# Moving two filler matmuls to another place within a step of the first attention's loop

## The chip, the cores and the metric

The kernel is written for one Trainium2 chip and runs on one of its cores. The metric is the device time of one execution in microseconds (us), and the figure for a kernel is the median of several executions. A profile is one further execution, recorded by the hardware profiler. The five engines named in it are TensorE (PE for its matmuls, PEld for its weight loads), VectorE (DVE), ScalarE (ACT), GpSimd (POOL) and SyncE (SP), which only issues transfers here. TensorE runs at one of two clock levels, 1.2 or 2.4 GHz. The profile gives the level that was granted as a share of the full one (1.00 or 0.50, or a mean of the two over a stretch).

## The reference

The reference is a decoder of two layers on 8 sequences of 128 tokens with 128 features. Each layer is a self-attention, a cross-attention to a context of 120 tokens, and a mixture of experts, each followed by a residual sum and a layer norm. The change is in the very first of these six parts, a differential attention with 16 heads of 8 features. Cut to what matters:

```
qkv = einsum('bnc,dc->bnd', x, W_qkv) split into q1, q2, k1, k2 (rotary) and v
attn1 = einsum('bhid,bhjd->bhij', q1, k1) * scale          # 8 sequences, 16 heads, 128 x 128
attn2 = einsum('bhid,bhjd->bhij', q2, k2) * scale
probs = softmax(attn1) - lam * softmax(attn2)
out   = einsum('bhij,bhjd->bhid', probs, v)                # then W_proj, residual, layer norm
```

## The kernel before

Nothing is scheduled by a planner. Each engine has its own program, written out by hand, and the engines meet at counting semaphores: an instruction adds to one when it ends, and another engine's program waits until the count is reached. What stands behind a wait on an engine's queue stands still with it.

The first attention works in 16 steps ("head numbers" n, 0 to 15). A step is a group of 16 score blocks of 128 x 128: four heads by four sequences, the four heads in the four 32-row quarters of TensorE. The names and lines that matter on TensorE's queue, in the order of one round n of the loop in `heads` (the function is printed below):

- `scores_t(n)` (lines 646 and 649): the transposed scores of step n, 16 matmuls of keys by queries (32 rows each) and 16 that add the row maxima. It waits until two score banks are free again (for the second, until DVE has taken the first half of the maxima of step n+2), and until ACT has copied the maxima of step n into `mT` (semaphore `mc`).
- `head_token(n-2)` (line 685): four 128 x 128 transposes of the finished outputs of step n-2 into the bank `BANK_M`.
- `head_values(n-1, 0)`: in the kernel before, first two fillers (line 607, in `keep_busy`), then the first eight matmuls of probabilities by values (line 673) into the bank `BANK_V`.
- `scores(n+2)` (line 633): the scores of step n+2 in the other orientation, 16 matmuls of 32 rows, from which DVE takes the row maxima.
- `head_maxima(n+1)` (line 660): one 128 x 128 transpose of the maxima of step n+1 into `BANK_M`.
- `head_values(n-1, 1)` (line 673): the second eight value matmuls.

A filler is a matmul of a 128 x 128 matrix of ones with 512 columns of ones (bf16). Its result is overwritten and used by nobody. In this loop only the first attention (`A`) has them; the second one (`D`), which runs through the same function later, adds masks with 128-row matmuls of 512 columns (line 622) instead.

The other engines in a round: DVE takes the row maxima in two halves (line 1318), cuts off their high bits (line 1326) and, in `finish_a` (lines 1342 to 1350), divides the outputs that `head_token` brought, which counts up `div`. POOL computes the low bits (line 506) and copies the values of a step (line 501). ACT runs, in this order, the two halves of the exponentials of step n, the copy of the maxima of step n+1 (into `mT`, counting up `mc`), and the copy of the outputs of step n-1 out of `BANK_V` (`outT`, counting up `ot`); all of ACT's work carries line 1072. SP loads queries and keys of later steps, eight steps ahead.

The last rounds differ: from n = 14 there are no `scores` left, from n = 15 no `head_maxima`, and the two rounds n = 16 and 17 only finish the outputs. Behind the loop `finish` issues five fillers of its own and goes on to the projection.

Of the kernel before, what the change touches and what calls it, by code (L numbers as in the profile page):

```python
# [48 lines left out]
BANK_V, BANK_M = 6, 7  # L49
# [80 lines left out]
def decoder_kernel(nc, d, out):  # L130
    with ExitStack() as ctx:
# [105 lines left out]
        def bank(n, k=1):  # L237
            return ps[:, n, :] if k == 1 else ps[:, n:n + k, :].rearrange("p a b -> p (a b)")
# [73 lines left out]
        A, D = Heads("a", 0), Heads("d", NH // RING)  # L312
# [288 lines left out]
        def _(pe):  # L601
            mm = nc.tensor.matmul

            def keep_busy(count, at):

                for _ in range(count):
                    mm(bank(at), onesb[:], fill, start=True, stop=True)  # L607
# [17 lines left out]
            def scores(a, n, causal):  # L625

                q, k = queries_of[n % RING], keys_of[n % RING]
                banks = head_banks(a, "s", n, causal, causS)
                for b in range(4):
                    cols = slice(b * P, (b + 1) * P)  # L630
                    for j in range(4):
                        rows = slice(QUAD * j, QUAD * j + QUAD)
                        last = mm(banks[j][:, cols], q[rows, cols], k[rows, cols], start=not causal, stop=not causal or b == 3)  # L633
                        if b == 3 and j % 2 == 1:
                            last.then_inc(a.s, 1)

            def scores_t(a, n, causal):

                q, k = queries_of[n % RING], keys_of[n % RING]
                banks = head_banks(a, "t", n, causal, causT)  # L640
                pe.wait_ge(a.mc, n + 1)
                for b in range(4):
                    cols = slice(b * P, (b + 1) * P)
                    for j in range(4):
                        rows = slice(QUAD * j, QUAD * j + QUAD)
                        mm(banks[j][:, cols], k[rows, cols], q[rows, cols], start=not causal, stop=False)  # L646
                    for j in range(4):
                        rows = slice(QUAD * j, QUAD * j + QUAD)
                        last = mm(banks[j][:, cols], pick[rows, b, :], mT[rows, n % 2, :], start=False, stop=not causal or b == 3)  # L649
                        if b == 3 and j % 2 == 1:  # L650
                            last.then_inc(a.st, 1)

            def head_maxima(a, n):

                pe.wait_ge(a.msplit, n + 1)
                if n >= 1:
                    pe.wait_ge(a.mc, n)
                if n >= 3:
                    pe.wait_ge(a.div, n - 2)
                nc.tensor.transpose(maxima_bank, mparts[:, n % 2].rearrange("p a b -> p (a b)"), ident).then_inc(a.mt, 1)  # L660

            def head_values(a, n, part):

                if part == 0:
                    pe.wait_ge(a.vs, n + 1)
                    if n >= 1:
                        pe.wait_ge(a.ot, n)
                    if a is A:
                        keep_busy(2, BANK_V)
                pe.wait_ge(a.exp, 2 * n + part + 1)  # L670
                for t in range(8 * part, 8 * part + 8):
                    j, k = divmod(t, 4)
                    last = mm(bank(BANK_V)[32 * k:32 * k + 32, j * P:(j + 1) * P], vs[:, n % 2, t, :], probs[:, n % 2, t, :],  # L673
                              start=True, stop=True)
                if part == 1:
                    last.then_inc(a.pv, 1)

            def head_token(a, n, count):

                pe.wait_ge(a.ot, n + 1)  # L680
                pe.wait_ge(a.mc, min(n + 3, count))
                if n >= 1:
                    pe.wait_ge(a.div, n)
                for k in range(4):
                    last = nc.tensor.transpose(bank(BANK_M)[:, k * P:(k + 1) * P], outT[:, k * P:(k + 1) * P], ident)  # L685
                last.then_inc(a.to, 1)

            def heads(a, count, causal):

                def loaded(n):  # L690
                    pe.wait_ge(a.stack[n % RING], (a.turns + n // RING + 1) * 16 * LOADS)

                for n in range(2):
                    loaded(n)
                    scores(a, n, causal)
                head_maxima(a, 0)
                for n in range(count + 2):
                    if n < count:
                        scores_t(a, n, causal)
                    if n >= 2:  # L700
                        head_token(a, n - 2, count)
                    if 0 <= n - 1 < count:
                        head_values(a, n - 1, 0)
                    if n + 2 < count:
                        loaded(n + 2)
                        scores(a, n + 2, causal)
                    if n + 1 < count:
                        head_maxima(a, n + 1)
                    if 0 <= n - 1 < count:
                        head_values(a, n - 1, 1)  # L710

            def finish(a, chunks, w):

                keep_busy(5, BANK_T)
                pe.wait_ge(a.norm, PAIRS)
                per = 4 // chunks
                banks = (BANK_S, BANK_S + 1, BANK_T, BANK_T + 1)
                for g in range(B // per):
                    for k in range(per):
                        for c in range(chunks):  # L720
                            o = bank(banks[g])[:, (k * chunks + c) * P:(k * chunks + c + 1) * P]
                            last = nc.tensor.transpose(o, oall[:, g * per + k, c * P:(c + 1) * P], ident)
                    last.then_inc(a.post, 1)
                for half in range(2):
                    pe.wait_ge(a.postc, (half + 1) * B // per // 2)
                    for k in range(4):
                        b = 4 * half + k
                        for c in range(chunks):
                            last = mm(bank(BANK_O + half)[:, k * P:(k + 1) * P], oT[:, b, c, :],
                                      w[:, c, :] if chunks == 2 else w[:],  # L730
                                      start=c == 0, stop=c == chunks - 1)
                    last.then_inc(a.y, 1)
# [44 lines left out]
            pe.wait_ge(fixed, 6)  # L777
            pe.wait_ge(tables, 5)
            heads(A, NH, causal=False)
            finish(A, 2, wproj0)  # L780
            keep_busy(10, BANK_T)
# [104 lines left out]
            pe.wait_ge(D.vall, 2)  # L886
            pe.wait_ge(D.full, 2)
            heads(D, PAIRS, causal=True)
            finish(D, 1, woD)

# [836 lines left out]
```

## Time and profile before

| | |
|---|---|
| three runs | 556.35, 557.04 and 563.35 us; median 557.04 us |
| profiled execution | 562.62 us, its span 560.8 us |
| mean granted clock over the span | 0.919 |
| busy share of the span | PE 87%, PEld 62%, DVE 50%, ACT 39%, POOL 18% |
| chain that ended last | PE 71%, DVE 18%, ACT 4%, DMA 2%, issue 2%, POOL 1% |

The profiled execution lies 5.58 us above the median, so a sum made in its own trace is made against 562.62 us. The chain that ended last is followed back from the last instruction: at each step to what released it, or to the instruction before it on the same engine. "Issue" is time in which an engine waited for nothing that the profile shows. The granted clock is read beside the busy share: TensorE can be busy all the time and yet work at half its speed.

### The profile page before, as it was taken

To read this page: it belongs to the slowest core of one execution; us is meant where nothing else is said; L and a number is where in the kernel's file an instruction comes from. 1 tells how busy PE (TensorE), PEld (TensorE's weight loads), DVE (VectorE), ACT (ScalarE), POOL (GpSimd) and SP (SyncE) were. 2 spreads that over 40 slices of the span, in tenths; PEclk is the share of its full clock that TensorE was granted. 3 is DMA by queue.
4 is the path that set the end of the run, shared out by engine and by line. 5 is a ranking of instruction groups with operands and counts; after the bars stand their busy time and mean duration, and the time that the engine had idled before them with its cause. 6 is when DMAs were issued, how large, how long until landed. Compare 5 with 4: busy or idle time off the path is not lost.

```text
span 560.8 us, 11515 instructions
## 1 busy us (share of the span) xinstructions
PE 487.8 (87%) x4512; PEld 347.0 (62%) x4512; DVE 283.2 (50%) x662; ACT 221.0 (39%) x359; POOL 101.5 (18%) x143
## 2 busy tenths in 40 slices
PE   8669988887689986789985899999998999999994
PEld 3456666664538953345563677777787667777774
DVE  2954566616764253334435966666614343333336
ACT  1324566641313300125432566666650643333330
POOL 2820112443100031000005222222221000000001
PEclk9865899998869998569997999999999999999998
DMA  7786430040400005700010000001000011111110
GB/s 202 254 289 212 137 107 2 3 152 0 151 0 1 1 1 213 255 6 3 2 40 12 12 13 13 13 21 28 2 1 1 20 28 39 38 38 38 38 28 37
DMA packets 23897, 34.36 MB, mean 61 GB/s; under 512 B 6400, under 2 KB 14544, under 8 KB 23600
## 3 DMA queue, kind: packets, MB, share of 16 engines
q1 hardware_dynamic: 23856, 33.77, 18.7%
q8 instruction: 31, 0.51, 0.4%
q14 instruction: 10, 0.08, 0.1%
HBM read 26.95 MB, written 6.82 MB: 60 GB/s over the span
## 4 chain that ended last, share of the span: by engine, by line
PE 71%; DVE 18%; ACT 4%; DMA 2%; issue 2%; POOL 1%; SPq 0%; POOLq 0%; DVEq 0%; ACTq 0%
PE ps L1024 10%; PE ps L1007 10%; PE ps L923 5%; DVE negm L1318 5%; PE ps L622 4%; PE ps L633 3%; PE ps L673 3%; PE ps L646 3%; PE ps L896 3%; PE ps L685 3%; PE ps L995 3%; PE ps L649 2%; PE ps L904 2%; PE ps L607 2%; PE ps L912 2%
## 5 line engine op out<-in xcount | busy, mean ns | idle before, releaser
L1318 DVE TENSOR_REDUCE negm<-ps 128x8 f32<-128x1024 f32 x48 | 56.5, 1219 | 55.1 <-PE ps L633 55.1
L1650 DVE SCALAR_TENSOR_TENSOR racc<-ps,sm,racc 128x128 f32<-128x128 f32 x128 | 35.9, 344 | 63.2 <-PE ps L1024 63.1
L1072 ACT ACTIVATE arena<-ps,w1a 128x512 f32<-128x512 f32 x64 | 43.4, 687 | 59.0 <-PE ps L1007 57.8
L1072 ACT ACTIVATE probs<-ps 128x1024 f32<-128x1024 f32 (+2 forms) x52 | 48.9, 989 | 39.7 <-PE ps L649 39.3
L1024 PEld LDWEIGHTS ps<-w1a,arena 128*128 128x128 f32 x512 | 59.4, 192 | 7.2 <-issue 6.2
L1024 PE MATMUL ps<-w1a,arena 128*128 128x128 f32 x512 | 59.8, 275 | 0.8 <-DVE racc L1641 0.8
L1007 PE MATMUL ps<-xT,w1a 128*128 128x512 f32 x128 | 58.0, 594 | 1.4 <-ACT xT L1072 1.4
L1072 ACT ACTIVATE arena<-ps 128x512 f32<-128x512 f32 (+4 forms) x62 | 35.1, 574 | 43.1 <-PE ps L831 15.8
L586 POOL TENSOR_TENSOR probs<-probs,rzE 128x480 f32<-128x480 f32 x32 | 30.6, 987 | 76.0 <-DVE rzE L1588 76.0
L545 POOL TENSOR_SCALAR rstd<-mv 128x4 f32<-128x4 f32 x12 | 2.7, 227 | 223.1 <-DVE mv L1379 223.1
L607 PE MATMUL ps<-onesb 128*128 128x512 bf16 x134 | 38.5, 424 | 3.0 <-DVE sm L1510 2.1
L1007 PEld LDWEIGHTS ps<-xT,w1a 128*128 128x128 f32 x128 | 23.0, 190 | 24.4 <-issue 22.2
L923 PEld LDWEIGHTS ps<-arena 128*128 128x128 f32 x256 | 30.4, 192 | 7.8 <-ACT arena L1072 4.2
L923 PE MATMUL ps<-arena 128*128 128x120 f32 x256 | 33.2, 278 | 1.6 <-ACT arena L1072 0.8
L673 PE MATMUL ps<-probs,vs 128*32 128x128 f32 x768 | 32.7, 296 | 0.0
L1575 DVE TENSOR_REDUCE negm<-ps 128x4 f32<-128x480 f32 x32 | 20.9, 654 | 20.8 <-PE ps L923 20.7
L506 POOL TENSOR_TENSOR mparts<-negm,mparts 128x64 f32<-128x64 f32 x24 | 7.7, 320 | 125.9 <-DVE mparts L1326 125.9
L649 PE MATMUL ps<-mT,pick 32*128 32x128 f32 x384 | 27.7, 306 | 0.0
L673 PEld LDWEIGHTS ps<-probs,vs 128*32 128x32 f32 x768 | 19.6, 115 | 12.1 <-issue 8.0
L1072 ACT ACTIVATE mT<-ps 128x128 fp32r<-128x128 f32 x24 | 6.7, 278 | 50.1 <-PE ps L660 50.1
L1072 ACT ACTIVATE probs<-probs 128x480 f32<-128x480 f32 x34 | 19.7, 600 | 13.1 <-DVE probs L1577 7.9
L1072 ACT ACTIVATE xT<-ps 128x512 f32<-128x512 f32 x10 | 6.0, 597 | 47.5 <-PE ps L738 47.4
(191 smaller groups left out, 836.3 us busy)
## 6 DMA issues: line engine op xcount, KB each, us to landing
stacks<-arena SPq DMA_DIRECT2D x12, 512.0 KB, 3.7
near<-stacks SPq DMA_DIRECT2D x12, 256.0 KB, 3.5
near<-stacks SPq DMA_DIRECT2D x24, 128.0 KB, 3.4
late<-stacks SPq DMA_DIRECT2D x12, 256.0 KB, 3.6
late<-stacks SPq DMA_DIRECT2D x24, 128.0 KB, 3.5
w1a<-in_w1a SPq DMA_DIRECT2D x1, 2048.0 KB, 7.5
w2a<-in_w2a SPq DMA_DIRECT2D x1, 2048.0 KB, 7.6
w1a<-in_w1b SPq DMA_DIRECT2D x16, 128.0 KB, 2.0
```

The lines of the kernel that those rows point to most:

```text
L586: nc.gpsimd.tensor_tensor(weights, weights, along(rzE[:, slot, 4 * g:4 * g + 4], L), ALU.mult).then_inc(e_norm, 1)
L607: mm(bank(at), onesb[:], fill, start=True, stop=True)
L622: mm(tiles(o, 4, P), identb[:], over(mask[:], 4), start=True, stop=False)
L649: last = mm(banks[j][:, cols], pick[rows, b, :], mT[rows, n % 2, :], start=False, stop=not causal or b == 3)
L673: last = mm(bank(BANK_V)[32 * k:32 * k + 32, j * P:(j + 1) * P], vs[:, n % 2, t, :], probs[:, n % 2, t, :], start=True, stop=True)
L923: last = mm(bank(BANK_S + g % 2)[:, k * L:(k + 1) * L], qz[:, slot, b, j, :], kE[:, slot, b * L:(b + 1) * L], start=True, stop=True)
L1007: mm(bank(BANK_S + u), w1s[:, slot, f * P:(f + 1) * P], xT[:, half * HALF:(half + 1) * HALF], start=True, stop=True).then_inc(g_up, 1)
L1024: last = mm(bank(banks + half)[:, k * P:(k + 1) * P], hid1[:, slot, f, b * P:(b + 1) * P], w2s[:, slot, f, :], start=f == 0, stop=f == F1 - 1)
L1072: return nc.scalar.activation(o, i, f, **kw)
L1318: nc.vector.tensor_reduce(negm[:, n % 2, 8 * h:8 * h + 8], pair_of(a.use, "s", n, h), AX.X, ALU.max, negate=True).then_inc(a.max, 1)
L1575: nc.vector.tensor_reduce(negm[:, slot, 4 * g:4 * g + 4], s, AX.X, ALU.max).then_inc(e_max, 1)
L1650: last = stt(racc[:, b, :], bank(banks + half)[:, k * P:(k + 1) * P], sm[:, 11, bass.ds(b * E1 + e, 1)], racc[:, b, :], ALU.mult, ALU.add)
```

## The change

The two fillers of a round leave their place ahead of the first value matmuls. They are issued behind the second value matmuls of the same round, ahead of the next round's `scores_t`, in the rounds 1 to 15 (before: 1 to 16). They write `BANK_M` in place of `BANK_V`. For that they wait until DVE has read the outputs that `head_token(n-2)` had put there (`div`), and until ACT has copied the maxima that `head_maxima(n+1)` had put there (`mc`).

```diff
                     pe.wait_ge(a.vs, n + 1)
                     if n >= 1:
                         pe.wait_ge(a.ot, n)
-                    if a is A:
-                        keep_busy(2, BANK_V)
                 pe.wait_ge(a.exp, 2 * n + part + 1)
...
                         head_maxima(a, n + 1)
                     if 0 <= n - 1 < count:
                         head_values(a, n - 1, 1)
+                    if a is A and 1 <= n < count:
+                        pe.wait_ge(a.div, n - 1)
+                        pe.wait_ge(a.mc, min(n + 2, count))
+                        keep_busy(2, BANK_M)
```

## Rows read from the trace of the kernel before

**Rows 1.** The page's 40 equal slices of the span: granted TensorE clock, in tenths.
```profile
PEclk9865899998869998569997999999999999999998
```

**Rows 2.** Stretches of the first attention's loop: length, busy us (instructions) by engine, clock.
```profile
core 0: us, PE busy (x) PEld busy (x) DVE busy (x) ACT busy (x) POOL busy (x), PEclk, DMA share, GB/s
31.70:41.36 9.66, 4.84 (x66) 3.88 (x67) 6.31 (x8) 2.49 (x4) 0.98 (x3) 0.59 0.91 310
41.36:47.78 6.42, 6.42 (x87) 4.29 (x87) 2.60 (x4) 2.22 (x3) 0.66 (x2) 0.50 0.85 275
47.78:55.08 7.30, 7.30 (x92) 5.11 (x91) 3.23 (x6) 2.81 (x4) 0.66 (x2) 0.50 0.47 159
55.08:60.67 5.59, 5.59 (x71) 4.16 (x70) 1.85 (x4) 2.54 (x3) 0.66 (x2) 0.50 0.75 244
62.26:108.92 46.66, 41.40 (x871) 30.02 (x871) 32.30 (x51) 28.15 (x41) 10.52 (x26) 1.00 0.16 48
```

**Rows 3.** Chain of waits, one round at full clock: start us, us, what.
```profile
90.25 0.33 PE ps L646 x4
...
91.37 0.59 PE ps L685 x4
91.96 0.43 PE ps L607 x2
92.39 0.57 PE ps L673 x16
92.96 0.66 PE ps L633 x16
93.62 1.22 DVE negm L1318
```

**Rows 4.** Timeline of that round: start us, us, engine line, tiles, idle before and releaser.
```profile
91.40 1.94 ACT L1072 ACTIVATE probs<-ps 128x1024 f32<-128x1024 f32 x2 [1.00 <-PE ps L649]
...
93.75 0.65 PE L673 MATMUL ps<-probs,vs 128*32 128x128 f32 x16
93.86 0.28 ACT L1072 ACTIVATE mT<-ps 128x128 fp32r<-128x128 f32 x1 [0.52 <-PE ps L660]
...
94.92 0.33 PE L646 MATMUL ps<-near 32*128 32x128 f32 x4 [0.53 <-DVE negm L1318]
```

**Rows 5.** Chain of waits, rounds n = 2 and 3, at half clock.
```profile
49.70 1.04 PE ps L685 x4
50.75 0.85 PE ps L607 x2
51.60 1.01 PE ps L673 x16
52.62 1.05 PE ps L633 x14
53.66 0.40 PE ps L660
54.07 1.01 PE ps L673 x16
...
57.00 1.04 PE ps L685 x4
```

**Rows 6.** Chain of waits, the loop's end (rounds 14 to 17).
```profile
111.63 0.26 PE ps L660
...
112.46 0.26 PE ps L646 x4
...
116.91 0.43 PE ps L607 x2
```

**Rows 7.** Timeline of TensorE in the second attention's loop, around 246 us.
```profile
244.99 1.08 PE L673 MATMUL ps<-probs,vs 128*32 128x128 f32 x16
246.26 1.86 PE L622 MATMUL ps<-causS,identb 128*128 128x512 bf16 x4 [0.20 <-ACT probs L1072]
```

**Rows 8.** Stretches around the second attention, columns as in rows 2.
```profile
221.20:248.30 27.10, 20.13 (x158) 10.17 (x162) 7.65 (x9) 4.43 (x6) 1.43 (x5) 0.50 0.51 162
248.50:299.50 51.00, 42.08 (x643) 27.39 (x639) 25.23 (x57) 21.88 (x33) 8.75 (x17) 1.00 0.04 12
```

## The prediction

> **What bounds the kernel now.** I read the 40 slices first. The granted clock is full for most of the span and low in the third and fourth slices, which is where the first attention's loop begins [rows 1]. So I cut that loop into stretches. Up to 41.36 us TensorE works only half of the time at a mostly low clock. From 41.36 to 60.67 us it is busy for every microsecond (6.42, 7.30 and 5.59 of the same) and yet at 0.50. From 62.26 to 108.92 us the clock is 1.00 and ten rounds take 46.66 us, 4.67 each [rows 2].
>
> Then the chain of waits in one round of each kind. At full clock it runs `scores_t` (90.25 to 91.37, 1.12 us), token transposes 0.59, fillers 0.43, first values 0.57, scores 0.66, DVE's first half of the maxima 1.22, and 0.08 until the next `scores_t` [rows 3]. TensorE's `head_maxima` (0.26) and second values are not on that chain: they run beside DVE, and TensorE then stands idle for 0.53 us until DVE lets it go [rows 4]. At half clock the same round is TensorE alone: `scores_t` 1.92 (47.78 to 49.70), transposes 1.04, fillers 0.85, values 1.01, scores 1.05, `head_maxima` 0.40, values 1.01, together 7.30 [rows 2, 5]. So the loop has two bounds: a path through DVE that contains the fillers when the clock is high, and TensorE's whole work, wherever the fillers stand, when it is low.
>
> **The change part by part, at a given clock.** *Fillers off the chain, full clock.* Ten rounds (n = 4 to 13) have 0.43 us of fillers between `scores_t` and the scores that DVE waits for [rows 3]. Without them a round is 4.67 - 0.43 = 4.24.
>
> *Fillers in the new place, full clock.* They go into the idle 0.53 [rows 4]. TensorE's work in a round is 1.12 + 0.59 + 0.57 + 0.66 + 0.26 + 0.57 + 0.43 = 4.20 [rows 3, 6], just under 4.24, so the cover is DVE's 1.22 and it is used up to the last 0.04; if a filler ran over, the next `scores_t` would be late by at most what is over, which I bound by 0 and 0.05 a round and take as 0. Ten rounds then give -4.3.
>
> *The added waits.* Behind the fillers stands the next `scores_t`, which waits for the same copy of the maxima anyway. Counted from the round's start, ACT's exponentials begin at 1.15 and take 1.94, and the copy (0.28) follows the transpose that ends at 3.20, so it ends at about 3.5; the second values end at about 3.7 [rows 4]. DVE's division comes much earlier. Cost 0. Only round 14 differs: it has no scores, TensorE gets through in 1.12 + 0.59 + 0.57 + 0.26 + 0.57 = 3.11, the copy behind the exponentials ends at 1.15 + 1.94 + 0.28 = 3.37, and 0.43 of fillers and some 0.05 of delay follow, 3.88 against the 3.54 between 108.92 and 112.46 [rows 2, 4, 6]: +0.34.
>
> *Bank and count.* Writing `BANK_M` in place of `BANK_V` takes the same time. Round 15's fillers go under ACT's exponentials and output copy, as they did before: 0. Round 16 has none now; they were on the chain [rows 6]: -0.43. No transfer is issued or moved past.
>
> *At half clock* the rounds n = 1 to 3 only change their order: 0.
>
> The sum at an unchanged clock is -4.3 + 0.34 - 0.43 = -4.4 us, 0.8%.
>
> **What the order does to the clock.** This is the term that decides, and the trace shows no run of it, so I bound it from both sides. The clock falls between 31.70 and 41.36 us, where TensorE waits for transfers and maxima [rows 2]; the change does not touch that. It rises again at 60.67 us. What had TensorE done? From 57.00 us the transposes, fillers and values had followed each other, 1.04 + 0.85 + 1.01 = 2.90 us of matmuls on all 128 rows, and then scores, which use 32 rows each [rows 5]. Round n = 2 had the same sequence from 49.70 to 52.62, and the clock stayed low [rows 2, 5]; so that sequence is no guarantee, and its place in time seems to count. But nothing weaker did it: `scores_t`, scores, `head_maxima` and the second values fill the rest of those 19 us without an idle moment, and the clock did not rise behind them. The second attention has no fillers there, and its clock rose at about 248.4 us, behind values of 1.08 us and masks of 1.86 us on 128 rows, 2.94 together but for a gap of 0.20 [rows 7, 8].
>
> The change breaks this sequence up. In the new order the 128-row work of a round at half clock comes as transposes and values, 1.04 + 1.01 = 2.05, then 1.05 of scores, then `head_maxima`, values and fillers, 0.40 + 1.01 + 0.85 = 2.26, then 1.92 of `scores_t`. Neither run comes to 2.90. Not until round 14, which has no scores, do they join: 1.04 + 1.01 + 0.40 + 1.01 + 0.85 = 4.31. So I expect the clock to stay low from the loop's beginning up to about the end of round 14.
>
> Price, in the profiled execution: round 1 stays 6.42, rounds 2 to 13 take 12 x 7.30 = 87.60, round 14 takes 1.92 + 4.31 = 6.23. The `scores_t` of round 15 then begins at 41.36 + 6.42 + 87.60 + 6.23 = 141.61 us, not at 112.46: +29.15 [rows 2, 5, 6]. Round 15 may begin at the low clock (up to 0.88 more for its `scores_t`; I take half) and round 16 saves 0.43: +29.2 in all. The other bound of this term is 0 (the clock rises at 60.67 as before), which leaves -4.4. I take the upper bound, because the new order's longest runs, 2.05 and 2.26, are nearer to the work that left the clock low.
>
> **Sum.** 562.62 + 29.2 = 591.8 us in the profiled execution's terms, 557.04 + 29.2 = 586.2 in the median's. The 5.58 us between the two may themselves be a clock that rose a round earlier (7.30 - 4.67 = 2.63 a round), a gain that the new order would lose again. I take the middle: 589.
>
> **Rivals.** *The clock rises as before* (faster side). TensorE is busy without a gap at half clock, before and after, so if that is what raises it, the order is nothing to it. For it: every rise in the loop came in busy time. Against it: 19 us of busy time from 41.36 us on without a rise [rows 2]. It decides if the full level is there by round 4. Time: 557.04 - 4.4 = 552.6. The Trainium skill says of this, in "TensorE: Matmul & The Clock Gate", Part 1, that throttled is the default and that activity releases it, and its practical advice is to leave no idle gaps; by that rule this rival's sum would stand, and those 19 us do not agree with a reading of activity as mere busy time.
>
> *The clock rises on the way*, by a favourable place in time, in one of the rounds 4 to 13. Each round then at full clock saves 7.30 - 4.24 = 3.06 on 589: a rise in round 8 gives 589 - 18 = 571.
>
> *The change does not do what it says*: the waits hold the fillers until the maxima's copy is late, and what leaves one place of the chain comes back in the other. Against it is the margin of 0.2 us between copy and values [rows 4]. The clock is as before; time 557.
>
> **Chances.** Clock low up to about round 14: 0.66, with its own range of 583 (the median's terms less one round at full clock) to 597 (low through round 15 and into the projection). A rise on the way: 0.12, two thirds of it above 568. As before: 0.17. No effect: 0.03. A rise earlier than before on top of the gain: 0.02. A measurement of this kernel can tell about 2% from no change, 545.9 to 568.2 us. Slower: 0.66 + 0.08 = 0.74; within: 0.04 + 0.17 + 0.03 = 0.24; faster: 0.02. The range 556 to 597 leaves out the faster cases, 0.19.
>
> **What would show it.** In the changed profile the granted clock of the stretch from 41 to about 140 us should read 0.50 with TensorE busy all of it, a round 7.30 us, fillers 0.85 a pair directly ahead of `scores_t`, and the clock should rise about where the scores end. Rounds of 4.24 us before that, with DVE's maxima still the releaser of `scores_t` and an idle time near 0.05 in place of 0.53, would make the forecast wrong and the first rival right; rounds of 4.67 the last one. A round at full clock clearly above 4.24 would show that the fillers run over.

## The result, and the profile after

The changed kernel takes 595.29 us (median of four runs, 589.37 to 597.32) against 557.42 us (four runs, 556.35 to 563.35): a ratio of 1.0646, with a 95% interval of 1.0554 to 1.0739. Ratios and intervals leave out executions that took over 1.5% more than the fastest of the same kernel; where there were some, their times are given. The changed kernel is slower, by about the size and for the reason that was forecast. The profiled execution took 597.32 us, its span is 595.5 us, and the mean granted clock fell from 0.919 to 0.847.

The page's slices of the changed kernel, granted clock in tenths, to be read beside [rows 1]:

```profile
PEclk9765555555985999955999699999999999999998
```

The low stretch that covered the third and fourth slices now reaches to the tenth (a slice is 14.9 us here). Stretches of the loop in the changed kernel, columns as in [rows 2]:

```profile
40.91:47.59 6.68, 6.49 (x87) 4.33 (x87) 3.58 (x4) 2.81 (x4) 0.66 (x2) 0.50 0.88 297
47.59:54.98 7.39, 7.39 (x91) 4.93 (x91) 3.23 (x6) 2.81 (x4) 0.66 (x2) 0.50 0.47 161
54.98:136.31 81.33, 81.33 (x962) 54.27 (x961) 35.57 (x56) 30.95 (x44) 11.14 (x28) 0.50 0.14 46
136.31:142.66 6.35, 6.35 (x75) 4.01 (x75) 0.89 (x4) 2.81 (x4) 3.70 (x7) 0.50 0.01 3
142.66:153.46 10.80, 8.67 (x116) 6.04 (x116) 2.05 (x6) 3.13 (x4) 4.02 (x6) 0.79 0.53 196
```

Eleven rounds fill the third row, 7.39 us each, and TensorE is busy in every microsecond of them at half clock. Where [rows 2] has ten rounds of 4.67 us, none of those rounds is at full clock now. The chain of waits of one such round in the changed kernel (start us, us, what; line 683 is the token transposes' line 685 of before, 671 the values' 673):

```profile
99.34 0.41 PE ps L646 x3
...
101.25 1.05 PE ps L683 x4
102.29 1.01 PE ps L671 x16
103.30 1.05 PE ps L633 x11
104.35 0.41 PE ps L660
104.76 1.01 PE ps L671 x16
105.77 0.97 PE ps L607 x2
106.74 0.40 PE ps L646
```

Beside [rows 5], nothing but the place of L607 and its time (0.97 for 0.85 us) is different: it stands behind the second values, and the chain never leaves TensorE. The longest run of 128-row matmuls is now 0.41 + 1.01 + 0.97 = 2.39 us (L660 to L607), where before it was 2.90. The end of the loop in the same chain:

```profile
138.21 1.04 PE ps L683 x4
139.26 1.01 PE ps L671 x16
140.27 0.41 PE ps L660
140.68 1.01 PE ps L671 x16
141.69 0.97 PE ps L607 x2
142.66 0.41 PE ps L646 x2
...
144.56 1.04 PE ps L683 x4
145.60 1.84 PE ps L671 x32
...
148.12 0.66 PE ps L683 x4
```

Round 14, without scores, puts 4.45 us of 128-row matmuls in a row, but the clock rises only at about 147.2 us, 4.5 us behind that run and 2.6 us into the next, in round 15's values: 32 of them take 1.84 us here and 1.05 us in the next round, and the transposes go from 1.04 to 0.66.

**Where the 34.7 us between the two profiled executions went.** The `scores_t` of round 15 starts 142.66 - 112.46 = 30.2 us later [rows 6]. From there to the first transpose of the projection it takes 10.80 us where it took 9.56 (112.46 to 122.02): 1.2 more, together 31.4. The other 3.3 us arise behind this attention, in parts that the change does not touch, where the clock was low for longer in this execution:

```profile
331.60:341.60 10.00, 8.10 (x23) 5.13 (x24) 2.81 (x6) 1.78 (x3) 2.52 (x2) 0.50 0.06 16
488.60:491.80 3.20, 3.20 (x17) 3.20 (x16) 1.89 (x7) 0.00 (x0) 0.00 (x0) 0.50 0.00 0
```

In the kernel before, the first was 6.6 us long (299.7 to 306.3), and from 306.5 to 555 the clock was full. Why it differed there was not tried.

### The profile page after: what moved, and what is told of

The parts are those of the page before. It is cut to its first block, busy times and chain, and to the rows that moved or that the text cites. A ratio compares the mean times of both kernels' runs of the same rounds, so it can differ in the third digit from the quotient of the medians.

```text
span 595.5 us, 11527 instructions
## 1 busy us (share of the span) xinstructions
PE 526.9 (88%) x4510; PEld 370.8 (62%) x4510; DVE 283.5 (48%) x662; ACT 221.1 (37%) x359; POOL 101.7 (17%) x143
## 4 chain that ended last, share of the span: by engine, by line
PE 74%; DVE 14%; ACT 4%; DMA 3%; issue 2%; POOL 2%; SPq 1%; POOLq 0%; DVEq 0%; ACTq 0%
PE ps L1026 10%; PE ps L1009 9%; PE ps L671 6%; PE ps L925 5%; PE ps L646 4%; PE ps L633 4%; PE ps L622 4%; PE ps L683 3%; PE ps L649 3%; PE ps L607 3%; PE ps L898 3%; PE ps L997 2%; DVE negm L1320 2%; PE ps L906 2%; PE ps L914 2%; PE ps L833 2%
## 5 line engine op out<-in xcount | busy, mean ns | idle before, releaser
L1026 PEld LDWEIGHTS ps<-w1a,arena 128*128 128x128 f32 x512 | 61.0, 196 | 7.2 <-issue 6.2
L1026 PE MATMUL ps<-w1a,arena 128*128 128x128 f32 x512 | 61.4, 280 | 0.8 <-DVE racc L1643 0.8
L607 PE MATMUL ps<-onesb 128*128 128x512 bf16 x132 | 42.2, 460 | 3.0 <-DVE sm L1512 2.1
L671 PE MATMUL ps<-probs,vs 128*32 128x128 f32 x768 | 43.6, 370 | 0.0
L925 PEld LDWEIGHTS ps<-arena 128*128 128x128 f32 x256 | 32.0, 200 | 7.5 <-ACT arena L1074 4.2
L649 PE MATMUL ps<-mT,pick 32*128 32x128 f32 x384 | 35.9, 375 | 0.0
L925 PE MATMUL ps<-arena 128*128 128x120 f32 x256 | 34.7, 286 | 1.3 <-ACT arena L1074 0.8
L671 PEld LDWEIGHTS ps<-probs,vs 128*32 128x32 f32 x768 | 25.3, 142 | 11.1 <-issue 9.1
L649 PEld LDWEIGHTS ps<-mT,pick 32*128 32x128 f32 x384 | 29.2, 293 | 0.0
L1344 DVE RECIPROCAL rz<-ps 128x16 f32<-128x16 f32 x16 | 4.1, 258 | 45.4 <-PE ps L683 45.4
```

The lines of the kernel that those rows point to most:

```text
L925: last = mm(bank(BANK_S + g % 2)[:, k * L:(k + 1) * L], qz[:, slot, b, j, :], kE[:, slot, b * L:(b + 1) * L], start=True, stop=True)
L1026: last = mm(bank(banks + half)[:, k * P:(k + 1) * P], hid1[:, slot, f, b * P:(b + 1) * P], w2s[:, slot, f, :], start=f == 0, stop=f == F1 - 1)
```

## The experiments

Two theories stood against each other. **Clock theory**: the new order takes apart the run of 128-row matmuls behind which the clock rose, and all else follows from the clock. **Wait and place theory**: the added waits, or the new place as such, make a round long.

### The waits without the move

```diff
                         head_values(a, n - 1, 1)
+                    if a is A and 1 <= n < count:
+                        pe.wait_ge(a.div, n - 1)
+                        pe.wait_ge(a.mc, min(n + 2, count))
```

> The fillers stay in their old place; only the two added waits (on the division and on the copy of the maxima) stand ahead of the next scores_t. Clock theory (the new order takes apart the run of 128-row matmuls behind which the clock rose): the order of the matmuls is that of before, so the clock rises in one of the rounds 2 to 6 and the time is that of before, 553 to 564 us, rounds of 4.67 us at full clock. Wait theory (the added waits themselves make the rounds long): about 595 us, at any rate above 570.

Measured: 561.81 us against 561.03 us of before on the same chip, ratio 1.0052 (1.0011 to 1.0093). The waits are not what costs 6%. But they are not free either. The chain of waits of one round at full clock:

```profile
91.11 1.22 DVE negm L1321
92.33 0.24 issue
92.58 0.33 PE ps L646 x4
...
93.69 0.59 PE ps L685 x4
```

Between DVE's maxima and `scores_t` there are now 0.24 us in which TensorE waits for nothing that the profile shows, where 0.08 stood before. (The maxima that `scores_t(n)` waits for are those of step n+1, not n+2 as listed ahead.) Rounds are 4.82 us, not 4.67.

### One of the two waits

```diff
+                    if a is A and 1 <= n < count:
+                        pe.wait_ge(a.div, n - 1)
```

> The fillers in the old place and one added wait alone (on the division). With both waits a round at full clock was 4.82 us in place of 4.67, 0.15 more, in an issue time behind DVE's maxima. If each wait costs TensorE's queue its own time: about 4.74 us. If it is the wait on the maxima's copy, which scores_t repeats: 4.67 us. If it is the first of the two: 4.82 us.

One execution, of 565.46 us. Its rounds take 4.82 us, with the same gap:

```profile
94.20 1.22 DVE negm L1320
95.42 0.25 issue
95.66 0.33 PE ps L646 x4
```

So the wait on the division costs 0.15 us a round, and the wait on the maxima's copy behind it nothing more. Whether that one would cost the same if it stood alone was not tried, and what TensorE's queue does in the 0.15 us is not shown.

### The fillers ahead of the tokens

```diff
+                    if a is A and 0 <= n - 1 < count:
+                        if n >= 2:
+                            pe.wait_ge(a.ot, n - 1)
+                        keep_busy(2, BANK_V)
                     if n >= 2:
                         head_token(a, n - 2, count)
...
-                    if a is A:
-                        keep_busy(2, BANK_V)
```

> The two fillers move the other way, ahead of the token transposes, and stay in the values' bank: fillers 0.85, transposes 1.04, values 1.01 are again 2.90 us of 128-row matmuls in one run at half clock. Clock theory: as before, 553 to 564 us, rounds of 4.67 us at full clock. Place theory (any place but the old one leaves the clock low): about 595 us.

Measured: 562.42 us, ratio 0.9992 (0.9938 to 1.0046). Another place in the round, a run of nearly the same length, and the time of before. But four of the eleven executions took 568.27 to 573.16 us, where three of 25 of before took 568.86 to 573.05. The profile is of one of the four, of 573.14 us, and shows a late rise: the clock was low up to about 82.0 us and full from there on, in rounds of 7.22 and then 4.62 us. The last run ahead of the rise, in the chain of waits, and the stretches (lines 683 and 671 are the transposes and the values):

```profile
78.34 0.96 PE ps L607 x2
79.31 0.85 PE ps L683 x4
80.16 1.01 PE ps L671 x16
```
```profile
33.40:83.50 50.10, 46.55 (x584) 33.26 (x584) 23.12 (x35) 19.18 (x28) 4.93 (x15) 0.52 0.52 174
83.60:119.60 36.00, 31.99 (x680) 23.66 (x680) 24.51 (x39) 22.01 (x32) 10.82 (x25) 1.00 0.06 17
```

The run lasts 2.83 us (78.34 to 81.17). It began in the same way at 49.46, 56.68, 63.90 and 71.12 us without a rise behind it, and the clock rose only behind the one from 78.34. When the clock rises differs between executions, and the times go with it: of the kernel before, 557.15 us came with a mean granted clock of 0.931, 562.65 with 0.919 and 573.05 with 0.900 (these means count the low stretches behind the loop too).

### Four fillers in the new place

```diff
-                        keep_busy(2, BANK_M)
+                        keep_busy(4, BANK_M)
```

> The changed kernel with four fillers in the new place in place of two. At half clock the run of 128-row matmuls there is 0.40 + 1.01 + 0.97 + 0.85 = 3.23 us. Clock theory: the clock rises in one of the first rounds; a round at full clock is then TensorE's work, 4.20 + 0.43 = 4.63 us; 553 to 568 us in all. Wait theory and place theory: the clock stays low, and 13 rounds are 0.85 us longer each than in the changed kernel: about 606 us.

Measured: 559.66 us, ratio 0.9994 (0.9949 to 1.004). More work in each round, in the same place and bank and behind the same waits, and the loss is gone. The chain of waits and two stretches of this kernel:

```profile
44.71 0.41 PE ps L660
45.11 1.01 PE ps L671 x16
46.13 1.82 PE ps L607 x4
...
49.37 0.59 PE ps L683 x4
```
```profile
31.70:48.60 16.90, 13.10 (x167) 9.39 (x167) 9.23 (x12) 5.30 (x8) 2.30 (x7) 0.50 0.88 297
48.80:109.20 60.40, 59.56 (x1129) 39.80 (x1125) 39.49 (x62) 36.48 (x52) 14.36 (x34) 1.00 0.24 74
```

The run is 0.41 + 1.01 + 1.82 = 3.24 us long, it ends at 47.95, and the clock is full by 48.8. So neither the new place nor its bank nor its waits keep the clock low by themselves. The two further fillers make the run longer and add 128-row work to the round; which of the two counts is not told apart here. The rounds at full clock take 4.72 us (53.05 to 57.77), 0.09 more than forecast.

### No fillers in the rounds

```diff
-                    if a is A and 1 <= n < count:
-                        pe.wait_ge(a.div, n - 1)
-                        pe.wait_ge(a.mc, min(n + 2, count))
-                        keep_busy(2, BANK_M)
```

> The changed kernel without the loop's fillers and without their waits. Clock theory: the clock stays low up to about round 14, and rounds 1 to 14 are shorter by the fillers' 0.97 us each: 595 - 14 = 581 us. Wait theory: without the waits the rounds run at full clock and at 4.24 us: about 552 us.

Measured: 578.99 us, ratio 1.0368 (1.028 to 1.0457). The rounds are 6.45 us, at half clock up to 129 us:

```profile
33.70:129.10 95.40, 92.36 (x1224) 69.24 (x1227) 46.76 (x71) 41.30 (x60) 16.55 (x42) 0.50 0.29 95
```

So in the changed kernel the fillers only cost: at half clock they bring a round from 6.45 to 7.39 us, and the clock rises no earlier for them (in round 15 of either kernel).

### Fillers in the new place only once the clock is up

```diff
-                    if a is A:
+                    if a is A and n < 6:
                         keep_busy(2, BANK_V)
...
+                    if a is A and 7 <= n < count:
+                        pe.wait_ge(a.div, n - 1)
+                        pe.wait_ge(a.mc, min(n + 2, count))
+                        keep_busy(2, BANK_M)
```

> Fillers in the old place in rounds 1 to 6, in the new place in rounds 7 to 15. Clock theory: the clock rises in rounds 2 to 6 as before and stays; seven rounds (7 to 13) at 4.24 in place of 4.67 us, less 0.1 us at the loop's end: 3 us less than before, 0.5%. Theory that the new place cannot hold a full clock: rounds of 7.39 us from 7 or 8 on, about 578 us.

Measured: 561.16 us, ratio 1.0009 (0.9958 to 1.0061). The 0.5% can't be told from nothing here. But the rounds can be read: 4.67 us in the old order and 4.34 in the new, and the new order keeps the clock:

```profile
73.74:104.10 30.36, 30.09 (x609) 20.86 (x610) 22.61 (x36) 19.70 (x29) 8.51 (x20) 1.00 0.08 24
```

The chain of waits of one such round:

```profile
92.20 0.59 PE ps L685 x4
92.79 0.57 PE ps L673 x16
93.36 0.04 issue
93.40 0.67 PE ps L633 x16
94.07 0.26 PE ps L660
94.33 0.57 PE ps L673 x16
94.91 0.54 PE ps L607 x2
95.44 0.28 PE ps L646
```

It is TensorE's from end to end; DVE's maxima are off it. The gain of a round is 0.33 us, not 0.43, because the pair of fillers takes 0.54 there and not 0.43 [rows 3].

### Early fillers in idle time, new place from round 1

Twenty-one fillers are added where TensorE stands idle ahead of round 1, to the changed kernel (`+` lines alone):

```diff
                     scores(a, n, causal)
+                    if a is A:
+                        keep_busy((6, 4)[n], BANK_V)
                 head_maxima(a, 0)
+                if a is A:
+                    keep_busy(2, BANK_V)
...
                         scores_t(a, n, causal)
+                        if a is A and n == 0:
+                            keep_busy(5, BANK_V)
...
                         head_maxima(a, n + 1)
+                        if a is A and n == 0:
+                            keep_busy(4, BANK_V)
```

> The changed kernel, and 21 more fillers (6, 4, 2, 5 and 4, into the values' bank) where TensorE stands idle ahead of round 1: behind each of the first two scores, behind the first transpose of maxima, behind the first scores_t and behind the maxima's transpose of round 0. Clock theory: the clock is full by round 1 or soon behind it, and then the new place does what it was to do: rounds of 4.24 us from there on, TensorE idle for hardly 0.05 us in each; some 12 us less than before, 545 to 554 us. If the new place or its waits are slow at any clock: rounds well above 4.67 us and no gain over before. If the clock falls back in the new order: about 595 us.

Measured: 551.52 us against 561.4; ratio 0.9814 (0.9757 to 0.9871). Five of the six executions took 547.3 to 553.26 us and one took 588.92. That one was profiled:

```profile
28.80:42.30 13.50, 12.43 (x178) 7.14 (x177) 7.83 (x10) 5.03 (x7) 2.95 (x6) 1.00 0.85 286
42.50:137.90 95.40, 95.40 (x1127) 63.55 (x1123) 41.54 (x65) 36.72 (x53) 14.81 (x36) 0.50 0.20 65
```

Here the clock was full, fell at about 42.4 us in round 1, and the new order did not bring it back for 95 us: both cases of the forecast in one kernel, 37 us apart. Rounds of the executions that kept the clock were not seen in a trace.

### Early fillers, none in the rounds

The same 21 fillers, and the four lines of the changed kernel taken out.

> As the kernel with 21 early fillers, but with none in the rounds. If the rounds hold the clock without fillers: rounds of 4.24 us, bound by the path through the maxima, 545 to 554 us. If the fillers of each round are what holds it: the clock falls in one of the first rounds, rounds of 6.42 us, about 575 us.

Measured: 579.57 us, ratio 1.0318 (1.0265 to 1.0372).

```profile
27.20:44.00 16.80, 13.37 (x198) 8.23 (x197) 10.39 (x14) 6.71 (x11) 4.65 (x7) 1.00 0.83 285
44.20:125.90 81.70, 81.70 (x1081) 61.12 (x1084) 40.47 (x64) 35.82 (x51) 14.39 (x36) 0.50 0.22 72
```

The clock fell at about 44.1 us, at the beginning of round 2, and stayed down for 82 us in which TensorE was never idle. The round before was the first of the loop's rounds without fillers at full clock, and TensorE was busy for 3.19 of its 4.34 us:

```profile
39.66:44.00 4.34, 3.19 (x81) 2.45 (x82) 2.55 (x4) 2.67 (x4) 0.66 (x2) 1.00 0.91 322
```

None of the six executions (574.25 to 580.23 us) came near the 547.3 to 553.26 of the five above. So the fillers in the rounds are wanted to hold the clock too, or to bring it back.

### Early fillers, old place in rounds 1 to 6 or in all

The 21 fillers in the kernel with the old place first, and in the kernel before.

> The 21 early fillers in TensorE's idle time ahead of round 1, then fillers in the old place in rounds 1 to 6 and in the new place in rounds 7 to 15. Clock theory: the old order holds the clock from round 1 on in every execution, so rounds 1 to 6 take 4.67 us and rounds 7 to 13 take 4.34 us (measured in the kernel with the old place first); the sum against before's profiled execution is some 9 us for the earlier clock and 2 us for the new place: 547 to 553 us, without the executions near 589 us of the kernel whose fillers are in the new place from round 1 on.

> The 21 early fillers and the fillers in the old place in all rounds. Clock theory: the clock is full from about round 1 on, rounds of 4.67 us; 549 to 555 us, 2 us more than with the new place from round 7 on. If it is the new place that gave the kernel with early fillers its gain: no change against before.

Measured, on one chip beside 561.17 us of before: 552.24 us, ratio 0.986 (0.9825 to 0.9895), and 552.49 us, ratio 0.9897 (0.9835 to 0.9959). Two of the first one's twelve executions took 558.07 and 565.34 us, and five of 17 of before 566.64 to 569.52. Both beat the kernel before by 1 to 1.4%, and the changed one by more, and the two cannot be told apart. In the second one's profile the clock is full through the whole loop, in rounds of 4.67 us:

```profile
41.00:110.00 69.00, 61.09 (x1285) 44.12 (x1278) 43.77 (x71) 41.88 (x59) 17.88 (x42) 1.00 0.36 118
```

The first one's profile is of an execution of 558.07 us in which the clock fell at 49.0 us, in round 3, while TensorE stood idle for 1.40 us within `scores_t` (from 48.08 us, for no reason that the profile shows), and rose again at 69.5: the old order does not hold the clock in every execution, though I had expected it to, but it brings it back.

## Why the prediction was right, point by point

**The order and the clock.** This was the term that decided, and it held. In the changed kernel the half clock lasts from before 41 to 147 us. That it is the clock and the order of the 128-row matmuls, and not the waits, the bank or the place as such, is shown from four sides: the waits alone change 0.5%, another place that leaves a run of 2.83 us takes the time of before, two more fillers in the new place take the loss back, and the new place after the clock is up gives 4.34 us a round. That it is the length of the run is argued, not shown. It is not enough by itself: 4.45 us in a row in round 14 of the changed kernel brought no rise, while 3.24 us with four fillers did, and runs of 2.83 us went by four times before one did. Why one run raises the clock and the same run a round earlier does not stays open.

**The price.** Forecast +29.2 us in the loop, measured +31.4. The rounds were mis-sized by 0.09 us (7.39 for 7.30): at half clock the pair of fillers took 0.97 in the new place and 0.85 in the old. And the rise came one round later than I had it: the joined run of round 14 did not bring it, and round 15's transposes and values were left at half clock. Round 15 cost 1.7 us more, where I had put 0.4; less the 0.43 of round 16's fillers that is the 1.2 us above. With the 3.3 us behind the loop, which stood in no term, and the middle taken between 586.2 and 591.8, the median is 6.3 us above the 589 forecast, inside the range and near its upper end of 597. The excess of the median over 557.42 is 37.9 us; the likeliest case had 589 - 557 = 32.

**The added waits, put at 0.** Wrong in size, though without weight here: 0.15 us a round where DVE's maxima are what `scores_t` waits for. The argument that `scores_t` waits for the same copy anyway looked at when the wait is met, not at what a further wait costs TensorE's queue. (The working for round 14 there adds up to 3.37 + 0.43 + 0.05 = 3.85 and not 3.88; the 0.03 us has no weight.)

**The gain at full clock, 0.43 a round.** It is 0.33. The step that failed is the bound of 0 to 0.05 for fillers that run over; the fillers were 0.11 longer in the new place, 0.04 of issue time came on top, and TensorE, not DVE, became the bound of the round.

**The rivals.** That busy time alone raises the clock is refuted twice more: 81.33 us in the changed kernel and 81.70 us with early fillers and none in the rounds, busy throughout, at 0.50. The Trainium skill gives the rule, in "TensorE: Matmul & The Clock Gate", Part 1, to leave TensorE no long idle gaps; these stretches have no gap at all, and the clock stayed low in them. A rise on the way was not seen in the four runs of the changed kernel, whose fastest, 589.37, leaves room for a round or two. That nothing would move is out.

## What to carry to other kernels

Matmuls that do nothing but keep TensorE's clock up are judged by the company that they stand in: moved out of a run of 128-row matmuls to a place where 32-row ones follow, meant for idle time, they cost 6%. Before such a move, read the granted clock by stretch, and ask for each stretch at half clock what raised it; here the idle time that was free at the high clock did not exist at the low one. The better place for such fillers was where TensorE waited anyway ahead of the loop (1 to 1.4%), with the fillers in the loop left where they raise the clock again.

## What the runs showed of the hardware

TensorE stood at 1.2 GHz through 95.4 us in which it was never idle, and without fillers in the rounds it fell from 2.4 to 1.2 GHz behind a round in which it was busy for 3.19 of 4.34 us, while with them rounds that were busy for 41.40 of 46.66 us kept it [rows 2]. One more wait ahead of a matmul, on a division that was done by then, cost 0.15 us a round behind another engine's release, and a second one behind it nothing. A pair of the same filler matmuls took 0.43 or 0.54 us at full clock, and 0.85 or 0.97 at half, by its place in the queue.
